# A state-space mixer with a quantized gate: the first chunk's norm token tile by token tile, the early loads in another order

## The chip, the cores and the metric

The kernel runs on one core of one Trainium2 chip. The core has five engines with queues of their own: TensorE (PE; PEld is its weight load), VectorE (DVE), ScalarE (ACT), GpSimd (POOL) and SyncE (SP), which here issues all DMA transfers of the program. The metric is the device time of one execution in microseconds (us), as the median of several runs.

## The reference

```python
xn = layernorm(x)                        # x is 1 x 2048 tokens x 1024
x_, gate = split(xn @ W_in.T)            # 2 x 2048 channels
u = silu(causal_conv4(x_) + conv_b)
ts, Bm, Cm = rms(split(u @ W_x.T))       # 64, 16 and 16 columns
dt = softplus(ts @ W_dt.T + b_dt)
state = state * exp(dt * A) + (dt * u) * Bm     # over the 2048 tokens, 16 states a channel
s = ((state . Cm) + u * D) * silu(gate) @ W_out.T
g = silu(ffn(xn))                        # int levels with scales, plus low rank gate_A, gate_B, ...
out = x + s * g
```

The change touches the layernorm of the first 512 tokens and the transfers around it. Everything behind is the same.

## The kernel before, in words

The kernel is written in raw instructions, one program for each engine, and each engine runs its program in the order in which it stands; semaphores (`f_...`, `z_...`) order engines against each other. SyncE's order of transfers is written out by hand. The program starts with a front part, up to about 549 us, and then a long scan.

The front part goes through four chunks of 512 tokens (four tiles of 128 tokens each) and in each chunk through 16 weight tiles of `W_in`; one (chunk, weight tile) is a unit, numbered u = 0 to 63, and every engine's loop runs over u. Before the loop, chunk 0 is prepared. VectorE takes the statistics of the four token tiles (`moments`), gathers them, and normalises (`scaled`) each tile; TensorE turns a tile in two halves (`turn_x`); ScalarE writes the turned half in half precision (`high`), and VectorE the rest that this leaves (`low`). `xn` has two buffers, the turned halves have two.

A weight tile w is loaded raw (`load_raw`, two buffers), scaled and rounded by ScalarE (`weight_high`, two instructions), its rest made by GpSimd (`weight_low`, counted in `f_lo`), used by TensorE in unit w, and stored to memory by SyncE (`store_w`), from where chunks 1 to 3 fetch it (`reload_w`). A raw buffer is free for tile w when `f_lo` says that w - 2 has been made. ScalarE's loop makes tile u + 2 first and then the tanh of unit u - 1; so a late raw tile also holds that tanh back. VectorE's loop is, for each u, `silu(u - 2)`, which waits for that tanh, then `conv(u - 1)`, then pieces for the next chunk's norm and the low-rank factors. The last instruction of a convolution adds three columns (L636). TensorE's loop is `unit(u)`, then `w_x(u - 2)`, which needs `silu(u - 2)`. GpSimd's `head` takes the seam between chunks from VectorE's convolutions, every fourth unit, ahead of `weight_low`.

SyncE's loop stores weight tile u + 2 and loads tile u + 4; at u = 0 it also loads x for chunk 1 (2 MB), at u = 14 it stores the low-rank factor table `b_s`, waits for it, and loads `wdt` behind it. The low-rank factors `lr_a` are loaded three times each (so many copies are needed side by side), `g_b` four times, each into 32 partitions.

In the profile's names, `dd` holds x and later `g_b` and `u_b`; `bb` holds `xn` and the raw weight tiles; `work` holds the converted weight tiles and the convolution's buffer; `inj` holds u, the constants and `lr_a`; `xtp_turned` are the turned halves, `main_decay` and `main_bank` the three result banks of the units; `xx` is the finished input of all units.

Of the kernel before, what the change touches and what calls it, by code (L numbers as in the profile page):

```python
# [27 lines left out]
ALU = mybir.AluOpType  # L28
# [3 lines left out]
P = 128  # L32
# [19 lines left out]
    "f_ds0 f_ds1 f_ww0 f_ww1 f_ww2 f_ws0 f_ws1 f_ws2 f_us0 f_us1 f_us2 f_dv f_ds2 f_tl "  # L52
# [30 lines left out]
def mixer_kernel(nc, x, win, convw, convb, wx, wdt, bdt, alog, dskip, wout, gu_q, g_scale, u_scale,  # L83
# [3 lines left out]
    with whole:  # L87
# [88 lines left out]
        with ExitStack() as st:  # L176
# [33 lines left out]
            rstd = sb(st, "rstd", [P, TPC, 1])  # L210
            bd = sb(st, "bd", [P, DT])
# [23 lines left out]
            f_us = [sem(f"f_us{b}") for b in range(3)]  # L235

# [41 lines left out]
            with nc.Block() as block:  # L278
                @block.sync
                def _(sp):  # L280
                    def load_x(c):
                        for half in range(2):
                            least(sp, f_xn, c * TPC - TPC + 2 * half + 2 if c else 0)
# [72 lines left out]
                    for w in range(2):  # L356
                        store_w(w)
                        load_raw(w + 2)
# [77 lines left out]
                def _(act):  # L436
# [8 lines left out]

                    def root(c):
                        act.wait_ge(f_nv, LEAD + 14 * c + 13)
                        act.activation(var[:, :, :], var[:, :, :], ACT.Sqrt).then_inc(f_sd, 1)
# [65 lines left out]
                    root(0)  # L514
                    for w in range(2):
                        weight_high(w)
                    for h in range(2 * TPC):
                        high(h)
                    for u in range(LAST + 2):
# [22 lines left out]
                        if u == 2:  # L542
                            act.wait_ge(f_const, LEAD + 112)
# [8 lines left out]
                        if u == 16:  # L552
                            act.wait_ge(f_const, LEAD + 144)
# [37 lines left out]
                def _(v):  # L591
                    def moments(c, t):
# [4 lines left out]
                    def gather(c):  # L597
                        v.wait_ge(f_nv, LEAD + 14 * c + 8)
                        for t in range(TPC):
                            v.bn_aggr(mv[:, t, :], stats[:, t, :, :].rearrange("p a s -> p (a s)")).then_inc(f_nv, 1)  # L600
                        v.wait_ge(f_nv, LEAD + 14 * c + 12)
                        v.tensor_scalar(var[:, :, :], mv[:, :, 1:2], 1e-5, None, ALU.add).then_inc(f_nv, 1)

                    def inverse(c):
                        v.wait_ge(f_sd, LEAD + c + 1)
                        v.reciprocal(rstd[:, :, :], var[:, :, :]).then_inc(f_nv, 1)

                    def scaled(c, t):
                        i = c * TPC + t
                        v.wait_ge(f_nv, LEAD + 14 * c + 14)  # L610
# [262 lines left out]
                def _(pe):  # L873
# [1126 lines left out]
```

## Time and profile before

| what | value |
|---|---|
| three runs | 2754.17, 2758.93, 2759.13 us |
| median | 2758.93 us |
| span of the profiled execution (first to last instruction) | 2757.4 us |
| busy over the span: TensorE, VectorE, GpSimd, ScalarE | 96%, 87%, 73%, 58% |
| mean granted clock of TensorE | 0.989 |

The profiled execution has no time of its own beside its span; the median stands 1.53 us above it, which is what lies around a span. Times in the rows count from the span's start. In a row of a timeline, the first number is the start, the second the time from the first to the last of the instructions that the row takes together, and what stands in brackets is how long the engine had been idle before, and what ended that.

### The profile page before, as it was taken

What the parts mean: (1) busy time and instruction counts of PE and PEld (TensorE: products, weight loads), DVE (VectorE), ACT (ScalarE), POOL (GpSimd) and SP (SyncE); (2) the same over time, 40 slices, a digit from 0 to 9 for tenths busy, and PEclk for the clock granted to TensorE, in tenths of its full rate; (3) what the DMA queues carried; (4) which work ended last, traced back from release to release, by engine and by line L of the source; (5) the groups of instructions that cost most, each with busy time, mean ns of one, the idle gap of its engine ahead of it and who ended that gap; (6) DMA issues with size and microseconds to landing.
All of it is one profiled execution on the core that took longest, in us unless ns stands there. A gap on an engine that the chain in (4) does not pass through costs nothing.

```text
span 2757.4 us, 41660 instructions
## 1 busy us (share of the span) xinstructions
PE 2653.1 (96%) x14980; PEld 1529.7 (55%) x14980; DVE 2392.3 (87%) x2900; ACT 1587.5 (58%) x2657; POOL 1999.2 (73%) x957
## 2 busy tenths in 40 slices
PE   6999999799999999999999999989999998999999
PEld 3545555355555555555555555556666665655644
DVE  5978877699999998888888888899999999999920
ACT  4444645666666666777777776655555555445500
POOL 2302223188999998888898988888999898999811
PEclk9999999899999999999999999999999999999999
DMA  7755476255565545454445445564565658666541
GB/s 246 239 173 193 141 268 210 100 161 177 157 194 172 161 135 160 130 156 138 150 124 166 130 126 161 169 198 120 156 157 133 165 128 254 163 175 192 149 128 58
DMA packets 338798, 449.10 MB, mean 163 GB/s; under 512 B 170592, under 2 KB 181088, under 8 KB 334496
## 3 DMA queue, kind: packets, MB, share of 16 engines
q1 hardware_dynamic: 338592, 446.43, 54.1%
q8 instruction: 120, 1.97, 0.3%
q14 instruction: 86, 0.70, 0.1%
HBM read 312.39 MB, written 133.96 MB: 162 GB/s over the span
## 4 chain that ended last, share of the span: by engine, by line
PE 34%; DVE 28%; issue 10%; DMA 3%; POOL 3%; ACT 1%; SPq 0%; DVEq 0%; POOLq 0%; ACTq 0%
DVE inj L1543 15%; DVE ysum L1563 9%; PE main_bank L1781 6%; PE main_bank L1783 6%; PE xtp_turned L1739 6%; PE main_bank L1857 4%; PE misc_bank L1781 3%; PE misc_bank L1783 3%; DMA h_s<-work 3%; PE misc_bank L1857 2%; POOL inj L1687 2%; DVE work L1597 1%; DMA gs_s<-work 1%; PE main_bank L1792 1%; DVE us L1572 1%
## 5 line engine op out<-in xcount | busy, mean ns | idle before, releaser
L1687 POOL TENSOR_TENSOR inj<-dd,bb 128x2048 f32<-128x2048 f32 x255 | 1156.4, 4535 | 181.0 <-PE xtp_turned L1739 179.7
L1739 PE MATMUL xtp_turned<-ident,inj 128*128 128x128 f32 x4096 | 626.3, 276 | 41.8 <-DVE inj L1543 31.1
L1543 DVE TENSOR_TENSOR_SCAN inj<-ssm_decay,carry,inj 128x512 f32<-128x512 f32 x512 | 655.8, 1281 | 4.1 <-ACT ssm_decay L1393 3.6
L1543 DVE TENSOR_TENSOR_SCAN inj<-main_decay,carry,inj 128x512 f32<-128x512 f32 x512 | 652.8, 1275 | 0.5 <-ACT main_decay L1393 0.3
L1739 PEld LDWEIGHTS xtp_turned<-ident,inj 128*128 128x128 f32 x4096 | 504.5, 142 | 253.0 <-DVE inj L1543 79.1
L1563 DVE SCALAR_TENSOR_TENSOR ysum<-xtp_turned,cT,ysum 128x512 f32<-128x512 f32 x707 | 522.6, 739 | 97.8 <-PE xtp_turned L1739 97.1
L1393 ACT ACTIVATE main_decay<-dd,aneg 128x512 f32<-128x512 f32 x511 | 351.1, 687 | 369.9 <-DVE inj L1543 369.5
L1393 ACT ACTIVATE ssm_decay<-dd,aneg 128x512 f32<-128x512 f32 x511 | 352.4, 690 | 282.7 <-DVE inj L1543 281.1
L1781 PE MATMUL main_bank<-xx,work 128*128 128x512 f16 x936 | 355.1, 379 | 2.4 <-ACT work L1406 2.4
L1783 PE MATMUL main_bank<-xx,work 128*128 128x512 f16 x936 | 355.2, 380 | 0.0
L1699 POOL TENSOR_TENSOR ysum<-ysum,work 128x512 f32<-128x512 f32 x239 | 306.2, 1281 | 10.5 <-ACT work L1439 10.5
L1762 PE MATMUL main_bank<-xx,work 128*128 128x512 f16 x960 | 234.8, 381 | 8.8 <-PEq L278 8.8
L894 PE MATMUL main_bank<-xx,work 128*128 128x512 f16 x1008 | 227.0, 382 | 4.3 <-DMA work<-w_s 4.1
L1439 ACT ACTIVATE work<-xtp_turned,cT 128x512 f32<-128x512 f32 x239 | 162.0, 678 | 63.9 <-POOL ysum L1699 39.6
L1857 PE MATMUL main_bank<-xx,work 128*128 128x512 f16 x768 | 186.0, 382 | 0.0
L1781 PE MATMUL misc_bank<-xx,work 128*128 128x512 f16 x472 | 179.3, 380 | 0.0
L1783 PE MATMUL misc_bank<-xx,work 128*128 128x512 f16 x472 | 179.1, 380 | 0.0
L894 PEld LDWEIGHTS main_bank<-xx,work 128*128 128x128 f16 x1008 | 97.6, 99 | 121.1 <-issue 8.2
L821 POOL TENSOR_TENSOR taps<-halo,inj 128x12 f32<-128x12 f32 x36 | 10.0, 304 | 200.5 <-DVE halo L633 200.5
L1762 PEld LDWEIGHTS main_bank<-xx,work 128*128 128x128 f16 x960 | 94.3, 98 | 88.8 <-issue 12.0
L1783 PEld LDWEIGHTS main_bank<-xx,work 128*128 128x128 f16 x936 | 91.7, 98 | 85.5 <-issue 0.3
L1781 PEld LDWEIGHTS main_bank<-xx,work 128*128 128x128 f16 x936 | 91.7, 98 | 85.4 <-ACT work L1406 2.6
(208 smaller groups left out, 3956.1 us busy)
## 6 DMA issues: line engine op xcount, KB each, us to landing
bb<-bt_s SPq DMA_DIRECT2D x128, 512.0 KB, 5.9
work<-w_s SPq DMA_DIRECT2D x48, 512.0 KB, 3.8
work<-in_gu_q SPq DMA_DIRECT2D x88, 256.0 KB, 3.4
h_s<-work SPq DMA_DIRECT2D x88, 256.0 KB, 3.8
u_s<-inj SPq DMA_DIRECT2D x64, 256.0 KB, 4.4
dd<-dt_s SPq DMA_DIRECT2D x32, 512.0 KB, 8.8
gs_s<-work SPq DMA_DIRECT2D x64, 256.0 KB, 6.1
us<-u_s SPq DMA_DIRECT2D x60, 256.0 KB, 5.4
```

Source lines behind the costliest of these rows:

```text
L894: mm = pe.matmul(main[u % 3][:, :], ww[:, u % 3, part, k * P:(k + 1) * P], xx[:, c, side, k, :], start=(k == 0 and part + side == 0), stop ...
L1393: act.activation(decay[j % 2][:, :], dtb[:, step % 2, j, :], ACT.Exp, scale=aneg[:, step % G * J + j, n:n + 1]).then_inc(s_dec, 1)
L1439: act.activation(ysum[:, step % 2, ADDS, :] if n == 0 else ev[:, :], turned[ADDS % 2][:, :], ACT.Copy, scale=cT[:, step // G * TPC + ADDS, ...
L1543: v.tensor_tensor_scan(inj[:, s % RING, j, :], decay[j % 2][:, :], inj[:, s % RING, j, :], carry[:, step % G * J + j, n:n + 1], ALU.mult, ...
L1563: v.scalar_tensor_tensor(dst, turned[t % 2][:, :], weight, dst, ALU.mult, ALU.add).then_inc(s_sum, 1)
L1687: pool.tensor_tensor(inj[:, e % RING, :, :], dub[:, step % 2, :, :], bb[:, e % 8:e % 8 + 1, :].broadcast_to([P, J, T]), ALU.mult).then_inc ...
L1699: pool.tensor_tensor(ysum[:, step % 2, ADDS, :], ysum[:, step % 2, ADDS, :], ev[:, :], ALU.add).then_inc(s_acc, 1)
L1739: mm = pe.transpose(turned[t % 2][:, j * P:(j + 1) * P], inj[:, s % RING, j, t * P:(t + 1) * P], ident[:, :])
L1762: mm = pe.matmul(bank[u % 3][:, :], gw[w % 2][:, part, h * P:(h + 1) * P], xx[:, c, side, h, :], start=(h == 0 and part + side == 0), stop ...
L1781: pe.matmul(dst[:, :], w, xx[:, p, 0, h, :], start=(h == 0), stop=False, skip_group_check=True)
L1783: mm = pe.matmul(dst[:, :], w, xx[:, p, 1, h, :], start=False, stop=False, skip_group_check=True)
L1857: mm = pe.matmul(bank[z % 3][:, :], y, (wo_hi, wo_hi, wo_lo)[w][:, i, half * T:(half + 1) * T], start=(i == 0 and w == 0), stop=(i == DT - ...
```

## The change

Chunk 0 is no longer normalised in one go. Its four tiles are loaded as two single tiles and a pair, each tile's mean and variance is taken when it has landed, and ScalarE normalises it, as x times the inverse deviation plus a shift, with VectorE making the shift (`first_...`). ScalarE's conversion of weight tile 0 stands between the tiles, that of tile 1 behind all of them. TensorE's first turn waits for the identity alone (`p_id`), not for all seven constants. In SyncE's order the low-rank loads `lr_a` stand in two groups around the first weight stores, and the `g_b` loads behind the load of raw tile 3. Chunks 1 to 3 are normalised as before; their counts are shifted by `NV0`.

```diff
-                    load_x(0)
-                    for w in range(2):
-                        load_raw(w)
-                    for dst, src in ((ident, ident_in), (wx_sb, wx), (cw, convw), (cb, convb), (bd, bdt), (al, alog),
-                                     (dsk, dskip)):
+                    load_first(0)
+                    load_first(1)
+                    sp.dma_start(ident[:], ident_in).then_inc(p_id, 16)
+                    load_raw(0)
+                    load_second()
+                    load_raw(1)
+                    for dst, src in ((cw, convw), (cb, convb), (bd, bdt), (al, alog), (dsk, dskip), (wx_sb, wx)):
                         sp.dma_start(dst[:], src).then_inc(f_const, 16)
-                    for m in range(2):
-                        for r in range(3):
-                            sp.dma_start(araw[:, m * HK:(m + 1) * HK, r * LR:(r + 1) * LR],
-                                         lr_a[m]).then_inc(f_a, 16)
+                    load_low_rank(0)
+                    store_w(0)
+                    load_raw(2)
+                    load_low_rank(1)
+                    store_w(1)
+                    load_raw(3)
                     for r in range(4):
                         sp.dma_start(braw[r * LR:(r + 1) * LR, :], g_b).then_inc(f_b, 16)
-                    for w in range(2):
-                        store_w(w)
-                        load_raw(w + 2)
...
+                    def first_scaled(t):
+                        act.wait_ge(f_nv, LEAD + first_done(t, "shift"))
+                        least(act, f_tp, 2 * t - 2)
+                        act.activation(xn[:, t % 2, :], xt[:, t, :], ACT.Identity, bias=shift[:, t, :],
+                                       scale=rstd[:, t, :]).then_inc(f_xn, 1)
...
-                    root(0)
-                    for w in range(2):
-                        weight_high(w)
-                    for h in range(2 * TPC):
-                        high(h)
+                    first_root(0)
+                    first_scaled(0)
+                    first_root(1)
+                    high(0)
+                    high(1)
+                    first_scaled(1)
+                    first_root(2)
+                    weight_high(0)
+                    high(2)
+                    high(3)
+                    first_scaled(2)
+                    first_root(3)
+                    high(4)
+                    high(5)
+                    first_scaled(3)
+                    high(6)
+                    high(7)
+                    weight_high(1)
...
-                    for t in range(TPC):
-                        moments(0, t)
-                    gather(0)
-                    inverse(0)
-                    scaled(0, 0)
-                    scaled(0, 1)
-                    for t in range(TPC):
-                        low(2 * t)
-                        low(2 * t + 1)
-                        if t + 2 < TPC:
-                            scaled(0, t + 2)
-                    v.wait_ge(f_const, LEAD + 112)
+                    first_moments(0)
+                    first_variance(0)
+                    for t in range(1, TPC):
+                        first_moments(t)
+                        first_inverse(t - 1)
+                        first_variance(t)
+                        if t > 1:
+                            low(2 * t - 4)
+                            low(2 * t - 3)
+                    first_inverse(TPC - 1)
+                    for h in range(2 * TPC - 4, 2 * TPC):
+                        low(h)
+                    v.wait_ge(f_const, LEAD + 96)
...
-                    pe.wait_ge(f_const, LEAD + 112)
+                    pe.wait_ge(p_id, LEAD + 16)
                     pe.wait_ge(f_z, LEAD + 1)
                     for h in range(2 * TPC):
                         turn_x(h)
+                    pe.wait_ge(f_const, LEAD + 96)
```

SyncE's queue, from the low-rank loads (`lr_a`, then `g_b`) to the load of raw weight tile 5, before; `w_s<-work` is a weight store, `bb<-in_win` a raw load:

```order
L352 DMA inj<-in_lr_a 128x8x32 x6
L355 DMA dd<-in_g_b 32x2816 x4
L294 DMA w_s<-work 128x2048 [waits f_lo]
L290 DMA bb<-in_win 128x1024 [waits f_lo]
L294 DMA w_s<-work 128x2048 [waits f_lo]
L290 DMA bb<-in_win 128x1024 [waits f_lo]
L294 DMA w_s<-work 128x2048 [waits f_lo]
L290 DMA bb<-in_win 128x1024 [waits f_lo]
L284 DMA dd<-in_x 128x2x1024 [waits f_xn] x2
L294 DMA w_s<-work 128x2048 [waits f_lo]
L290 DMA bb<-in_win 128x1024 [waits f_lo]
```

The same stretch of the changed kernel:

```order
L298 DMA inj<-in_lr_a 128x8x32 x3
L314 DMA w_s<-work 128x2048 [waits f_lo]
L310 DMA bb<-in_win 128x1024 [waits f_lo]
L298 DMA inj<-in_lr_a 128x8x32 x3
L314 DMA w_s<-work 128x2048 [waits f_lo]
L310 DMA bb<-in_win 128x1024 [waits f_lo]
L379 DMA dd<-in_g_b 32x2816 x4
L314 DMA w_s<-work 128x2048 [waits f_lo]
L310 DMA bb<-in_win 128x1024 [waits f_lo]
L304 DMA dd<-in_x 128x2x1024 [waits f_xn] x2
L314 DMA w_s<-work 128x2048 [waits f_lo]
L310 DMA bb<-in_win 128x1024 [waits f_lo]
```

The `g_b` loads have moved behind two weight stores and two raw loads that wait for `f_lo`, so they stand directly ahead of store 2, raw load 4, x of chunk 1, store 3 and raw load 5.

ScalarE ahead of its loop, before; L439 and L444 are the two instructions of `weight_high`, L453 is `high`:

```order
L448 ACTIVATE var<-var 128x4 [waits f_nv]
L439 ACTIVATE bb<-bb 128x1024 [waits f_w0]
L444 ACTIVATE work<-bb 128x1024 [waits f_sc]
L439 ACTIVATE bb<-bb 128x1024 [waits f_w1]
L444 ACTIVATE work<-bb 128x1024 [waits f_sc]
L453 ACTIVATE xx<-xtp_turned 128x4x128 [waits f_tp] x8
```

The changed kernel, from the normalising of token tile 1 (L474; L469 is the root) to the conversion of weight tile 1:

```order
L474 ACTIVATE bb<-dd,shift,rstd 128x1024 [waits f_nv]
L469 ACTIVATE rstd<-var 128x1 [waits f_nv]
L460 ACTIVATE bb<-bb 128x1024 [waits f_w0]
L465 ACTIVATE work<-bb 128x1024 [waits f_sc]
L484 ACTIVATE xx<-xtp_turned 128x4x128 [waits f_tp] x2
L474 ACTIVATE bb<-dd,shift,rstd 128x1024 [waits f_tp,f_nv]
L469 ACTIVATE rstd<-var 128x1 [waits f_nv]
L484 ACTIVATE xx<-xtp_turned 128x4x128 [waits f_tp] x2
L474 ACTIVATE bb<-dd,shift,rstd 128x1024 [waits f_tp,f_nv]
L484 ACTIVATE xx<-xtp_turned 128x4x128 [waits f_tp] x2
L460 ACTIVATE bb<-bb 128x1024 [waits f_w1]
L465 ACTIVATE work<-bb 128x1024 [waits f_sc]
```

Both weight conversions have moved from ahead of the turned halves to among and behind them.

## Rows read from the trace of the kernel before

**Rows 1.** Stretches: us; busy PE, PEld, DVE, ACT, POOL; clock; DMA share, GB/s.

```profile
54.00:120.00 66.00, 66.00 (x363) 37.47 (x362) 61.25 (x96) 40.43 (x45) 29.25 (x26) 1.00 0.70 229
120.00:150.00 30.00, 25.65 (x127) 13.56 (x125) 20.84 (x35) 5.37 (x8) 0.97 (x5) 0.89 0.89 290
150.00:480.00 330.00, 330.00 (x1713) 174.09 (x1712) 268.99 (x454) 171.63 (x218) 78.60 (x56) 1.00 0.59 192
```

**Rows 2.** Timeline, TensorE: start, us, line, output<-inputs, count, idle before.

```profile
19.02 1.97 PE L879 MATMUL xtp_turned<-ident,bb 128*128 128x128 f32 x8 [19.02 <-DMA dsk<-in_dskip]
...
30.27 7.25 PE L894 MATMUL main_decay<-xx,work 128*128 128x512 f16 x24 [1.51 <-DVE xx L619]
...
79.01 5.34 PE L894 MATMUL main_bank<-xx,work 128*128 128x512 f16 x24
...
141.58 7.92 PE L894 MATMUL main_bank<-xx,work 128*128 128x512 f16 x24 [4.13 <-DMA work<-w_s]
```

**Rows 3.** Timeline, SyncE's queue, the DMA issues.

```profile
10.28 10.10 SPq L352 DMA_DIRECT2D inj<-in_lr_a  x6
20.42 2.18 SPq L355 DMA_DIRECT2D dd<-in_g_b  x4
...
37.20 0.33 SPq L294 DMA_DIRECT2D w_s<-work  x1
...
41.23 0.56 SPq L290 DMA_DIRECT2D bb<-in_win  x1
...
122.28 0.32 SPq L298 DMA_DIRECT2D work<-w_s  x1
...
130.75 1.37 SPq L396 DMA_DIRECT2D inj<-in_wdt  x2
132.16 0.92 SPq L298 DMA_DIRECT2D work<-w_s  x1
```

**Rows 4.** Timeline, GpSimd, weight subtraction.

```profile
70.85 2.13 POOL L809 TENSOR_TENSOR work<-bb,work 128x1024 f16<-128x1024 f32 x1 [5.50 <-ACT work L444]
...
115.28 4.22 POOL L809 TENSOR_TENSOR work<-bb,work 128x1024 f16<-128x1024 f32 x2
```

**Rows 5.** Timeline, VectorE.

```profile
9.82 5.04 DVE L595 BATCH_NORM_STATS2 stats<-dd 128x6 f32<-128x512 f32 x8 [4.62 <-DMA dd<-in_x]
...
29.43 0.69 DVE L619 TENSOR_TENSOR xx<-xtp_turned,xx 128x512 f16<-128x512 f32 x1 [0.16 <-ACT xx L453]
...
54.02 0.69 DVE L643 SCALAR_TENSOR_TENSOR inj<-main_bank,work 128x512 f32<-128x512 f32 x1 [2.74 <-ACT main_bank L458]
...
71.02 1.98 DVE L636 TENSOR_TENSOR work<-work,corr 128x3 f32<-128x3 f32 x1
...
76.14 0.69 DVE L643 SCALAR_TENSOR_TENSOR inj<-main_bank,work 128x512 f32<-128x512 f32 x1
```

**Rows 6.** Timeline, ScalarE.

```profile
15.56 0.20 ACT L448 ACTIVATE var<-var 128x4 f32<-128x4 f32 x1 [9.74 <-DVE var L602]
...
20.17 0.60 ACT L453 ACTIVATE xx<-xtp_turned 128x512 f16<-128x512 f32 x1 [0.33 <-PE xtp_turned L879]
21.02 0.60 ACT L453 ACTIVATE xx<-xtp_turned 128x512 f16<-128x512 f32 x1 [0.26 <-PE xtp_turned L879]
...
41.88 1.06 ACT L439 ACTIVATE bb<-bb 128x1024 f32<-128x1024 f32 x1 [0.26 <-DMA bb<-in_win]
...
51.27 1.06 ACT L439 ACTIVATE bb<-bb 128x1024 f32<-128x1024 f32 x1 [3.41 <-DMA bb<-in_win]
...
53.40 0.58 ACT L458 ACTIVATE main_bank<-work 128x512 f32<-128x512 f32 x1
```

**Rows 7.** Stretches, columns as in the first group: the `g_b` loads, then plain loads.

```profile
22.00:28.50 6.50, 5.20 (x24) 3.92 (x22) 4.55 (x7) 2.94 (x5) 0.10 (x1) 1.00 1.06 225
30.00:34.00 4.00, 3.73 (x9) 1.31 (x10) 0.39 (x4) 1.14 (x2) 0.00 (x0) 1.00 1.02 418
```

**Rows 8.** One stretch, line 636 alone: us, VectorE's busy time, clock, DMA.

```profile
54.00:120.00 66.00, 5.97 (x10) 1.00 0.70 229
```

More of the change, by code:

```diff
@@ L210, in mixer_kernel @@
             rstd = sb(st, "rstd", [P, TPC, 1])
+            shift = sb(st, "shift", [P, TPC, 1])
             bd = sb(st, "bd", [P, DT])
@@ L235, in mixer_kernel, with first_done @@
             f_us = [sem(f"f_us{b}") for b in range(3)]
+            p_id, p_x = sem("p_id"), sem("p_x")
+            def first_done(t, what):
+                last = 6 * t + 5 + 2 * (t < TPC - 1)
+                return {"stats": 6 * t, "mean": 6 * t + 3, "var": 6 * t + 4, "inverse": last, "shift": last + 1}[what]
+            NV0 = first_done(TPC - 1, "shift")
             def least(eng, s_, count):
@@ L280, in _, with load_first, load_second, load_low_rank @@
                 def _(sp):
+                    def load_first(t):
+                        sp.dma_start(xt[:, t, :], x[t]).then_inc(f_x[t], 16)
+                    def load_second():
+                        sp.dma_start(xt[:, 2:4, :], x[2:4].rearrange("t p h -> p t h")).then_inc(p_x, 16)
+                    def load_low_rank(m):
+                        for r in range(3):
+                            sp.dma_start(araw[:, m * HK:(m + 1) * HK, r * LR:(r + 1) * LR],
+                                         lr_a[m]).then_inc(f_a, 16)
                     def load_x(c):
                         for half in range(2):
-                            least(sp, f_xn, c * TPC - TPC + 2 * half + 2 if c else 0)
+                            least(sp, f_xn, c * TPC - TPC + 2 * half + 2)
                             sp.dma_start(xt[:, 2 * half:2 * half + 2, :],
@@ L444, in weight_high, with first_root @@
                         act.activation(ww[:, w % 3, 0, :], wraw[:, w % 2, :], ACT.Copy).then_inc(f_hi, 1)
+                    def first_root(t):
+                        act.wait_ge(f_nv, LEAD + first_done(t, "var"))
+                        act.activation(rstd[:, t, :], var[:, t, :], ACT.Sqrt).then_inc(f_sd, 1)
+                    def first_scaled(t):
[3 more added lines that the diff above has]
+                                       scale=rstd[:, t, :]).then_inc(f_xn, 1)
                     def root(c):
-                        act.wait_ge(f_nv, LEAD + 14 * c + 13)
+                        act.wait_ge(f_nv, LEAD + NV0 + 14 * (c - 1) + 13)
                         act.activation(var[:, :, :], var[:, :, :], ACT.Sqrt).then_inc(f_sd, 1)
@@ L552, in _ @@
                         if u == 16:
-                            act.wait_ge(f_const, LEAD + 144)
+                            act.wait_ge(f_const, LEAD + 128)
                             act.wait_ge(f_bs, LEAD + 48)
@@ L591, in _, with first_moments, first_variance, first_inverse @@
                 def _(v):
+                    def first_moments(t):
+                        v.wait_ge(f_x[t] if t < 2 else p_x, LEAD + 16)
+                        for h in range(2):
+                            v.bn_stats(stats[:, t, h, :], xt[:, t, h * 512:(h + 1) * 512]).then_inc(f_nv, 1)
+                    def first_variance(t):
+                        v.wait_ge(f_nv, LEAD + max(2, first_done(t, "stats")))
+                        v.bn_aggr(mv[:, t, :], stats[:, t, :, :].rearrange("p a s -> p (a s)")).then_inc(f_nv, 1)
+                        v.wait_ge(f_nv, LEAD + first_done(t, "mean"))
+                        v.tensor_scalar(var[:, t, :], mv[:, t, 1:2], 1e-5, None, ALU.add).then_inc(f_nv, 1)
+                    def first_inverse(t):
+                        v.wait_ge(f_sd, LEAD + t + 1)
+                        v.reciprocal(rstd[:, t, :], rstd[:, t, :]).then_inc(f_nv, 1)
+                        v.wait_ge(f_nv, LEAD + first_done(t, "inverse"))
+                        v.tensor_scalar(shift[:, t, :], mv[:, t, 0:1], rstd[:, t, :], -1.0, ALU.mult, ALU.mult
+                                        ).then_inc(f_nv, 1)
                     def moments(c, t):
@@ L609, in scaled @@
                         i = c * TPC + t
-                        v.wait_ge(f_nv, LEAD + 14 * c + 14)
+                        v.wait_ge(f_nv, LEAD + NV0 + 14 * (c - 1) + 14)
                         least(v, f_tp, 2 * i - 2)
```

10 lines of the change are left out of this document (5 added, 5 removed).

## Prediction

> **What bounds the kernel now.** I read the table of stretches first, because this change touches only the first microseconds and the question is whether their end is handed on. From 150 to 480 us TensorE is busy for all 330 us [rows 1], so what lies behind 150 us starts as early or as late as TensorE gets into that stretch, and a shift there goes to the end one for one. Between 54 and 120 us TensorE is also busy throughout, but VectorE is busy for 61.25 of 66 us [rows 1]. Two engines look like the limit at once, and which of them is decides this case.
>
> The TensorE rows tell. Unit 0 (the first weight tile) starts at 30.27, and unit 17 at 141.58 after 4.13 us of waiting for the weight tile that `reload_w` fetches [rows 2]. So TensorE arrives early there; its lead is thrown away. I then followed what that reload waited for, backwards. In SyncE's queue it is issued at 132.16, behind the `wdt` loads at 130.75, which wait for the `b_s` stores, which stand behind the first reload at 122.28 [rows 3]; that one waits until all 16 weight tiles are stored, and the last two are made by GpSimd at 115.28 to 119.50, right behind `head` [rows 4], whose input is a VectorE convolution. So the chain runs through VectorE, and it is VectorE's pace from 54 us on that sets unit 17, not TensorE's.
>
> Where does VectorE's full stretch begin? At 54.02, after 2.74 us of idling for ScalarE's tanh of unit 2 [rows 5]. That tanh, at 53.40, stands on ScalarE behind `weight_high(5)`, which began at 51.27 after 3.41 us of waiting for the load of raw tile 5 [rows 6]. So the transfer that lands at 51.27 starts the chain. It was issued at 41.23, and with it queued, from 37.20 on, two stores, two weight loads and the 2 MB of x for chunk 1 [rows 3].
>
> **The change, step by step.** *The head.* Before, 1 MB of x had landed at 9.82 and eight statistics took 5.04 us [rows 5]. A 0.52 MB tile at the 418 GB/s of a full read stretch [rows 7] is 1.25 us less: tile 0 at 8.57. Two statistics 1.26, aggregate and variance 0.4, root 0.20 [rows 6], then, behind tile 1's statistics on VectorE, reciprocal and shift near 11.95. Normalising on ScalarE is a 128x1024 operation not in the trace in this form; the nearest is the copy with a scale at 1.06 [rows 6]; two 128x512 operations of 0.60 [rows 6] give 1.20 from above, and nothing cheaper of that size is there. I take 1.05. So TensorE turns the first half tile at 13.05, not 19.02 [rows 2]; the constants it waited for are no longer in its way.
>
> From there ScalarE sets the pace, since it now normalises, converts and makes weight tile 0 between. A turned half is ready 1.15 us after its start and a second 0.85 later (19.02 to 20.17 to 21.02 [rows 2, 6]): high(0) and high(1) 14.2 to 15.65, normalise tile 1 to 16.7, root 16.9, `weight_high(0)` two operations, 19.05; high(2), high(3) 20.25; tile 2 21.3, root 21.5; turned halves at 22.5 and 23.35, done 23.95; tile 3 25.0; halves from 26.15, done 27.6. VectorE's low part is 0.69 [rows 5]: unit 0 starts near 28.45, 1.8 us earlier. The second x transfer (behind 0.59 MB more, at the latest 13.75) is covered. The new 128x1 operations are under 0.2 us each and lie in this sum.
>
> *What moved behind it.* `weight_high(1)` now stands after high(7): 27.6 to 29.75, GpSimd's 2.13 [rows 4] to 31.95. Only then may SyncE issue `store_w(1)` and the load of raw tile 3, and behind them the four `g_b` loads, which in the old queue were issued at 20.42 [rows 3]. Store and load of a tile on an idle queue took from 37.20 to 41.88, 4.68 us [rows 3, 6]: raw tile 3 lands at 36.65. ScalarE and GpSimd make tile 3 of it by 41.1; before, `store_w(3)` and load 5 began with 41.23, so their place in the queue is the same.
>
> But the queue is longer. The `g_b` copies are 4 x 352 KB into 32 partitions each; the stretch in which they move has the engines full at 225 GB/s, where full-width transfers have 418 [rows 7]: 1.44 MB / 0.225 = 6.4 us. Before, they were done while TensorE still turned chunk 0. Now they move between load 3 and the chain's five transfers. These took 51.27 - 37.20 = 14.07 us with an empty queue, of which some 2.05 are issue and landing (4.68 less 1.05 MB at about 0.4): 12.0 of moving. Load 5 lands at 36.65 + 6.4 + 12.0 = 55.05 instead of 51.27: **+3.8 us**.
>
> *Handed on.* Tanh of unit 2 at 57.2, VectorE's full stretch from 57.8. VectorE has at most 66 - 61.25 = 4.75 us of gaps in its 66 [rows 1], mostly its wait for the tanh of the unit it has just convolved, so it does not catch up. ScalarE's and GpSimd's weight tiles, and the loads behind them, follow VectorE's units; unit 17 moves by the same 3.8. TensorE's 1.8 us of lead is used up: its `w_x(5)` after unit 7, just ahead of unit 8 at 79.01 and with silu(5) done at 76.83 [rows 2, 5], now waits until 80.6, and unit 8 starts near 81.6. Nothing else is lost, as its margin to unit 17 is 4.13 us.
>
> The small rest costs nothing at the end: three low-rank loads each ahead of `store_w(0)` and `store_w(1)` are issued while those wait (all six took 10.10 us of issue [rows 3], three of them fit between 22.1 and 31.95); the constants land long before unit 0; VectorE loses four normalisations, but before 28 us.
>
> Sum: -1.8 at unit 0, not handed on; +6.4 for `g_b` in the chain's queue, less 2.6 by which the way is free earlier (37.20 + 2.05 for issue and landing, against 36.65); net +3.8 us. The profiled execution spans 2757.4 us, 1.53 under the median of the three runs, 2758.93; I add the difference to the median: **2762.7 us**, +0.14%. What a measurement of this kernel can tell is about 0.2%, 5.5 us; so my forecast counts as no change.
>
> **Bounds.** `g_b` at the full 418 GB/s would be 3.4 us: the sum is then +0.8. If normalising is 1.20 and tile 0 lands only with the whole megabyte, the head is 1.7 us later, and the sum +5.5.
>
> **Rivals.** *The lead arrives.* If transfers from different requests share the engines instead of following each other, load 5 is not late, tanh 2 follows convolution 2, and the start's 1.8 us go through: 2757.1. Against it: load 4, with 2 MB of x issued right behind it, still landed by 41.88, 4.68 us after the store ahead of it was issued [rows 3, 6], and load 5, behind the 2 MB, took until 51.27. Chance 0.13.
>
> *The clock pays back.* The wait before unit 17 is followed by half clock: that unit took 7.92 us where a unit at full clock takes 5.34 [rows 2], and the granted clock of the stretch is 0.89 [rows 1]. If the new wait at unit 8 already drops the clock to 1.2 GHz, TensorE arrives at unit 17 with less to wait, and the drop there may not come: 3.8 - 2.6 = +1.2, 2760.1. Chance 0.13.
>
> *Slower.* VectorE's three-column addition L636 takes 0.16 us, but 1.98 at 71.02, ending at 73.00, when GpSimd's weight subtraction from 70.85 ends (72.98) [rows 4, 5]. Ten of them between 54 and 120 us take 5.97 [rows 8], 4.4 over 10 x 0.16. Since loads now land at other times, the subtractions can meet more of the additions; from 1.7 us more on (one full meeting) the kernel is over 0.2% slower, and twice the meetings give 3.8 + 4.4 = +8.2, 2767.1. Against it: both sides hang on VectorE's units, so the meetings should recur. Chance 0.17, and the same rows allow -0.6 if there are none. The Trainium skill, "SBUF — State Buffer", section "Who interferes with whom", says a VectorE instruction with two SBUF inputs and a GpSimd instruction that reads SBUF lock each other out, the later one blocked until the first has ended. By that rule each addition issued inside a subtraction waits for its end, so that the sum hangs on the offset alone; the trace agrees, with 73.00 against 72.98.
>
> **How the numbers follow.** Forecast +3.8: 0.54; the other three as given; 0.03 for anything else. Its own range is 2759.7 to 2764.4 from the bounds. Eight in ten need the clock and the start rival and half the lock's reach, and the runs' own spread (2754.17 to 2759.13): 2755.5 to 2767.5. Faster by over 0.2% needs the start's gain and no meeting at all: 0.05. Slower by over 0.2%: the lock's 0.17 and the forecast's upper edge, 0.23. Same: 0.72.
>
> **What would show it.** Right: unit 0 at 27.5 to 29.5; ScalarE waits for raw tile 5 until 54 to 56; a TensorE wait behind unit 7; unit 17 near 145.4. Wrong: load 5 at or before 51.3, with `g_b` beside it; unit 17 earlier than 141.58; or a unit 0 after 30, which would mean that ScalarE's row in the head is longer than I made it.

## The result and the profile after

| | before | changed |
|---|---|---|
| median, 22 runs each on the same chip | 2758.62 us | 2763.91 us |
| lowest to highest | 2753.18 to 2764.01 us | 2758.68 to 2769.92 us |
| span of the profiled execution | 2757.4 us | 2757.8 us |
| mean granted clock of TensorE | 0.989 | 0.989 |

The ratio is 1.002, 95% interval 1.0013 to 1.0027: 5.3 us slower, at the edge of what was called no change. The forecast was 2762.7 us, +3.8, and lies inside the interval too. The two spans differ by 0.4 us only; below it is read what became of the difference in them. All medians and ratios here and in the experiments leave out the five slow executions of the later sessions, which took from 4202 to 13432 us.

The changed kernel's timeline of TensorE, with the columns of [rows 2]: two of the four turnings of the head, unit 0, the `w_x` ahead of unit 8, units 8, 17 and 63:

```profile
12.93 1.94 PE L942 MATMUL xtp_turned<-ident,bb 128*128 128x128 f32 x8 [12.93 <-ACT bb L474]
17.93 1.97 PE L942 MATMUL xtp_turned<-ident,bb 128*128 128x128 f32 x8 [3.06 <-ACT bb L474]
...
29.41 7.86 PE L957 MATMUL main_decay<-xx,work 128*128 128x512 f16 x24 [1.50 <-DVE xx L681]
...
81.24 1.13 PE L968 MATMUL ssm_decay<-work,inj 128*128 128x96 f32 x8 [2.67 <-DVE inj L705]
82.21 7.03 PE L957 MATMUL main_bank<-xx,work 128*128 128x512 f16 x24
...
146.65 7.04 PE L957 MATMUL main_bank<-xx,work 128*128 128x512 f16 x24 [4.12 <-DMA work<-w_s]
...
477.76 5.34 PE L957 MATMUL main_decay<-xx,work 128*128 128x512 f16 x24
```

Against [rows 2] the first turning is 6.1 us earlier, unit 0 only 0.86, unit 8 3.2 us later and unit 17 5.07 later. Unit 63, the last of the front part, is the best place to see what is handed on; before, it stood here:

```profile
473.57 5.34 PE L894 MATMUL main_decay<-xx,work 128*128 128x512 f16 x24
```

That is 4.19 us and not 5.07, since unit 17 took 7.04 us, not 7.92: less of it ran at half clock (granted clock 0.76 over the unit, 0.66 before).

ScalarE's timeline of the changed kernel, as [rows 6]: the normalising of tiles 0 and 1, raw weight tiles 3 and 5, the tanh of unit 2, raw tile 13:

```profile
11.55 1.24 ACT L474 ACTIVATE bb<-dd,shift,rstd 128x1024 f32<-128x1024 f32 x1 [1.30 <-DVE shift L651]
...
16.63 1.24 ACT L474 ACTIVATE bb<-dd,shift,rstd 128x1024 f32<-128x1024 f32 x1 [1.13 <-DVE shift L651]
...
39.02 1.06 ACT L460 ACTIVATE bb<-bb 128x1024 f32<-128x1024 f32 x1 [6.41 <-DMA bb<-in_win]
...
55.54 1.06 ACT L460 ACTIVATE bb<-bb 128x1024 f32<-128x1024 f32 x1 [3.95 <-DMA bb<-in_win]
...
57.68 0.58 ACT L489 ACTIVATE main_bank<-work 128x512 f32<-128x512 f32 x1
...
106.24 1.06 ACT L460 ACTIVATE bb<-bb 128x1024 f32<-128x1024 f32 x1 [0.96 <-DMA bb<-in_win]
```

Raw tile 5 lands at 55.54 where it landed at 51.27, and the tanh stands right behind its conversion, as before. VectorE, as [rows 5]: the statistics of token tile 2, the shift of tile 1 and silu of unit 2:

```profile
15.00 1.29 DVE L639 BATCH_NORM_STATS2 stats<-dd 128x6 f32<-128x512 f32 x2 [3.19 <-DMA dd<-in_x]
16.20 0.15 DVE L649 RECIPROCAL rstd<-rstd 128x1 f32<-128x1 f32 x1
16.38 0.21 DVE L651 TENSOR_SCALAR shift<-mv,rstd 128x1 f32<-128x1 f32 x1
...
58.29 0.69 DVE L705 SCALAR_TENSOR_TENSOR inj<-main_bank,work 128x512 f32<-128x512 f32 x1 [3.59 <-ACT main_bank L489]
```

SyncE's queue, as [rows 3]: store 1, load 3, `g_b`, store 2; then the reload of unit 16, the second `b_s` store, `wdt`, the reload of unit 17:

```profile
32.81 0.33 SPq L314 DMA_DIRECT2D w_s<-work  x1
33.18 0.43 SPq L310 DMA_DIRECT2D bb<-in_win  x1
33.66 2.26 SPq L379 DMA_DIRECT2D dd<-in_g_b  x4
35.96 0.66 SPq L314 DMA_DIRECT2D w_s<-work  x1
...
127.48 0.33 SPq L318 DMA_DIRECT2D work<-w_s  x1
...
128.95 0.66 SPq L414 DMA_DIRECT2D b_s<-ab  x1
135.97 1.38 SPq L417 DMA_DIRECT2D inj<-in_wdt  x2
137.39 1.01 SPq L318 DMA_DIRECT2D work<-w_s  x1
```

The stretches, with the columns of [rows 1]:

```profile
54.00:120.00 66.00, 63.00 (x335) 34.79 (x335) 57.77 (x92) 40.65 (x45) 25.17 (x23) 0.97 0.73 236
120.00:150.00 30.00, 25.46 (x132) 13.85 (x131) 25.82 (x42) 7.66 (x11) 5.48 (x9) 0.95 0.81 253
150.00:480.00 330.00, 330.00 (x1710) 173.84 (x1709) 267.95 (x450) 168.78 (x216) 75.43 (x55) 1.00 0.59 194
```

TensorE now has 3.0 us of idling between 54 and 120 us, and from 150 to 480 it is full again: the shift of 4.19 is carried through it unchanged. Behind it the two profiled executions differ, and no row shows why. After a wait of 1.07 us near 490 the execution of before got half clock for a few products (0.57 granted from 491 to 495 us), and six of them took 2.74 us; the changed one took 1.47 for the same six and made up 1.6 us there. Before:

```profile
491.25 0.38 PE L927 MATMUL misc_back<-inj 128*128 128x512 f16 x1 [1.07 <-DVE inj L676]
491.56 0.61 PE L928 MATMUL misc_back<-inj 64*128 64x512 f16 x1
492.10 2.74 PE L940 MATMUL xtp_turned<-xx,a 128*128 128x512 f16 x6
```

Of the kernels below only one (`w1_early`) drops there too. That leaves 2.57 us at the first GpSimd product of the scan (551.78 us, 549.21 before), and the scans take up most of that, so that the spans end 0.4 us apart. A single pair of spans is therefore no measure of a change of this size; the medians are.

### The profile page after: what moved, and what is told of

Same layout as the page of the kernel before. It is cut to its first block, busy times and chain, and to the rows that moved or that the text cites. A ratio compares the mean times of both kernels' runs of the same rounds, so it can differ in the third digit from the quotient of the medians.

```text
span 2757.8 us, 41676 instructions
## 1 busy us (share of the span) xinstructions
PE 2654.5 (96%) x14980; PEld 1530.6 (56%) x14980; DVE 2392.1 (87%) x2906; ACT 1591.7 (58%) x2664; POOL 1999.3 (72%) x957
## 4 chain that ended last, share of the span: by engine, by line
PE 34%; DVE 29%; issue 11%; POOL 3%; DMA 3%; ACT 1%; DVEq 0%; SPq 0%; POOLq 0%; ACTq 0%
DVE inj L1607 15%; DVE ysum L1627 9%; PE main_bank L1845 6%; PE main_bank L1847 6%; PE xtp_turned L1803 6%; PE main_bank L1921 4%; PE misc_bank L1847 3%; PE misc_bank L1845 3%; DMA h_s<-work 2%; PE misc_bank L1921 2%; POOL inj L1751 2%; DVE work L1661 1%; PE main_bank L1856 1%; DVE us L1636 1%; DVE xa L1672 1%
```

## The experiments

My theory after the result: the `g_b` loads in the queue of raw tiles 4 and 5 make raw tile 5 late, this holds the tanh of unit 2 and with it VectorE, and VectorE's lateness goes through the weight stores to unit 17. Rivals: that the late start of the head or of weight tile 1 is what counts, or the place of `g_b` alone, or that unit 17 would be late anyway. All experiments ran in three sessions, each with runs of the kernel before; its medians there were 2757.09 us (35 runs), 2755.84 (32) and 2757.07 (27). Each experiment has 10 or 11 runs. The last three columns are starts in the profiled execution (of raw tile 5, that of its conversion on ScalarE). The ratio is to the runs of before in the same session; kernels of different sessions are compared by it and not by their medians.

| kernel | median us | ratio to before, interval | raw tile 5 | unit 17 | unit 63 |
|---|---|---|---|---|---|
| before | 2758.62 | | 51.27 | 141.58 | 473.57 |
| changed | 2763.91 | 1.002 [1.0013, 1.0027] | 55.54 | 146.65 | 477.76 |
| gb_early | 2756.81 | 0.9999 [0.999, 1.0007] | 49.93 | 140.68 | 472.47 |
| old_gb_late | 2755.51 | 0.9995 [0.9986, 1.0003] | 48.50 | 139.38 | 470.66 |
| gb_wide | 2759.53 | 1.0008 [1.0, 1.0017] | 53.16 | 144.22 | 475.24 |
| tanh_first | 2760.38 | 1.0013 [1.0004, 1.0022] | 55.67 | 143.97 | 475.54 |
| w1_early | 2756.69 | 1.0001 [0.9992, 1.001] | 51.15 | 142.26 | 474.29 |
| pair_first | 2762.02 | 1.0016 [1.0007, 1.0025] | 55.22 | 145.64 | 476.39 |
| reload_early | 2761.88 | 1.0024 [1.0015, 1.0034] | 54.98 | 141.22 | 478.61 |
| three | 2757.74 | 1.0005 [0.9996, 1.0014] | 52.20 | 137.25 | 473.28 |
| wdt_late | 2758.49 | 1.0008 [0.9999, 1.0017] | 55.80 | 142.20 | 474.75 |
| gb_wdt | 2753.76 | 0.9992 [0.9983, 1.0001] | 49.85 | 137.13 | 469.91 |
| old_wdt | 2754.97 | 0.9993 [0.9984, 1.0002] | 51.36 | 137.13 | 469.51 |

The starts are those of one execution each. `tanh_first`, `reload_early` and `wdt_late` have the same transfers as the changed kernel up to raw tile 5, and there it starts at 55.67, 54.98 and 55.80: less than 1 us between two kernels shows nothing in that column.

**gb_early.** The changed kernel with `g_b` back ahead of the first weight store, all else as changed.

```diff
                     load_low_rank(0)
+                    for r in range(4):
+                        sp.dma_start(braw[r * LR:(r + 1) * LR, :], g_b).then_inc(f_b, 16)
                     store_w(0)
...
                     load_raw(3)
-                    for r in range(4):
-                        sp.dma_start(braw[r * LR:(r + 1) * LR, :], g_b).then_inc(f_b, 16)
```

> The changed kernel with the four g_b loads moved forward in SyncE's queue, directly behind the first low-rank loads and ahead of store_w(0). Theory (g_b stands in the way of the five transfers whose last one is raw tile 5): g_b is then moved before 29 us, raw tile 5 lands near 49.5 instead of 55.54, tanh of unit 2 near 51.5 to 52, no TensorE wait behind unit 7 of more than 1 us, unit 17 at 139 to 141 instead of 146.65, and the time 5 to 7 us under the changed kernel's, 0 to 2 us under the kernel before. Rival (the head alone is at fault, since ScalarE makes weight tile 1 only behind the last turned half, so that every later weight tile is late): raw tile 5 still lands after 54, unit 17 stays at 145 to 147, and the time stays 4 to 6 us above the kernel before.

The whole loss is gone with this one line's place. ScalarE's timeline in it, raw tile 5 and the tanh of unit 2:

```profile
49.93 1.06 ACT L460 ACTIVATE bb<-bb 128x1024 f32<-128x1024 f32 x1 [1.63 <-DMA bb<-in_win]
...
52.07 0.58 ACT L489 ACTIVATE main_bank<-work 128x512 f32<-128x512 f32 x1
```

Raw tile 5 lands 5.61 us earlier than in the changed kernel, unit 17 is 5.97 earlier, unit 63 5.29, although unit 0 starts at 29.99, 0.58 later than in the changed kernel. So what the head gains does not reach unit 17, and what the queue loses does.

**old_gb_late.** The kernel before with `g_b` behind the load of raw tile 3, that is, only this part of the change.

```diff
-                    for r in range(4):
-                        sp.dma_start(braw[r * LR:(r + 1) * LR, :], g_b).then_inc(f_b, 16)
                     for w in range(2):
                         store_w(w)
                         load_raw(w + 2)
+                    for r in range(4):
+                        sp.dma_start(braw[r * LR:(r + 1) * LR, :], g_b).then_inc(f_b, 16)
```

> The kernel before with one edit alone: the four g_b loads stand behind the load of raw tile 3, as in the changed kernel. There that load is issued at 24.6 us and not after 32.8. Theory (only bytes that are still in the queue when store 2 is issued count): raw tiles 2 and 3 land about 5 us earlier, g_b is moved from 29 to 35.5, ahead of the chain's transfers, which are issued from about 34 instead of 37.2; raw tile 5 lands at 48 to 50 instead of 51.27, unit 17 at 139 to 141 instead of 141.58, the time 0 to 2.5 us under the kernel before. Rival (the place behind raw tile 3 costs g_b's 6.4 us whatever the head is): raw tile 5 at 54 to 56, unit 17 at 145 to 147, the time 4 to 6 us above the kernel before.

So the place in the order of the program doesn't cost by itself. Here weight tiles 0 and 1 are made early, the `g_b` loads are issued at 23.19 and have moved before store 2 is issued at 33.80. The loss needs both: `g_b` behind raw tile 3, and weight tile 1 made late, so that `g_b` is issued at 33.66, 2.3 us ahead of store 2. Raw tile 5 is converted here without a wait, and the tanh of unit 2 waits for its convolution, not for a transfer. Raw tiles 2 and 3 are converted 3.4 and 2.3 us earlier than before (29.44 and 32.97), not the 5 expected. ScalarE, raw tile 5 and the tanh:

```profile
48.50 1.04 ACT L439 ACTIVATE bb<-bb 128x1024 f32<-128x1024 f32 x1
...
52.98 0.60 ACT L458 ACTIVATE main_bank<-work 128x512 f32<-128x512 f32 x1 [2.26 <-DVE work L636]
```

**w1_early.** The changed kernel with the conversion of weight tile 1 right behind that of tile 0.

```diff
                     weight_high(0)
+                    weight_high(1)
...
                     high(7)
-                    weight_high(1)
```

> The changed kernel with one edit on ScalarE: the conversion of weight tile 1 stands right behind that of tile 0, between the turned halves of token tile 0 and 1, instead of behind the last half. SyncE's order is as it was. Theory (what counts is when g_b's bytes leave the queue ahead of the chain's transfers): store_w(1), raw load 3 and g_b are issued from about 27 instead of 32.8, g_b is through by 38 instead of 43, raw tile 5 lands at 50 to 51.5, unit 17 at 140.5 to 142.5 instead of 146.65, and the time is 4 to 6 us under the changed kernel's, although unit 0 starts 1.5 to 2.1 us later (31 to 31.5). Rival (TensorE's start is what is handed on): unit 17 and the time move with unit 0, 1.5 to 2 us later than in the changed kernel.

This is the plainest of the runs. Unit 0 starts at 31.79, 2.4 us later than in the changed kernel and 1.5 later than before, and the kernel is still as fast as before. Store 1 is issued at 27.30 and `g_b` at 28.47 instead of 33.66, and raw tile 5 lands at 51.15 (51.27 before). TensorE's early start is not handed on; the place in the queue is. Unit 0 and raw tile 5 in it:

```profile
31.79 6.88 PE L957 MATMUL main_decay<-xx,work 128*128 128x512 f16 x24 [1.50 <-DVE xx L681]
```
```profile
51.15 1.06 ACT L460 ACTIVATE bb<-bb 128x1024 f32<-128x1024 f32 x1 [1.85 <-DMA bb<-in_win]
```

**gb_wide.** The changed kernel, with `g_b` stored four times over in memory, prepared outside the kernel, and loaded as four column pieces into 128 partitions each: as many bytes and as many transfers as in the changed kernel, but full width.

```diff
-                        sp.dma_start(braw[r * LR:(r + 1) * LR, :], g_b).then_inc(f_b, 16)
+                        cut = slice(r * IPAD // 4, (r + 1) * IPAD // 4)
+                        sp.dma_start(braw[:, cut], g_b[:, cut]).then_inc(f_b, 16)
```

> The changed kernel with g_b repeated four times in memory by the host and loaded in four column pieces into all 128 partitions, the same 1.44 MB and the same place in the queue. Theory (32 partitions are why g_b moves at 225 GB/s): it moves at 380 to 420 GB/s in 3.4 to 3.8 us instead of 6.4, raw tile 5 lands 2.6 to 3 us earlier (52.5 to 53), unit 17 at 143.5 to 144.5, the time 2.5 to 3.5 us under the changed kernel's. Rival (g_b is slow for another reason, such as the mixture of stores and loads around it): no change, raw tile 5 near 55.5, unit 17 near 146.6.

ScalarE's timeline in it, raw tiles 3 and 5:

```profile
37.49 1.06 ACT L461 ACTIVATE bb<-bb 128x1024 f32<-128x1024 f32 x1 [5.01 <-DMA bb<-in_win]
...
53.16 1.06 ACT L461 ACTIVATE bb<-bb 128x1024 f32<-128x1024 f32 x1 [3.94 <-DMA bb<-in_win]
```

Of the 5.61 us that `g_b` costs raw tile 5, 2.38 are due to the 32 partitions; the bounds of the prediction (6.4 and 3.4) had 3.0 for it. Between 38 and 43 us, behind raw tile 3, the transfers run at 340 GB/s here; the changed kernel has 211 from 38 to 43.5. The Trainium skill, "SBUF — State Buffer", section "Door 1: The DMA port swizzle (why `[64,N]` ≈ `[32,N]`)", says that partitions 0 to 31 reach 8 of the 16 ports and gives about 218 GB/s for them, 436 for all; the trace agrees, with 225 and 418 [rows 7].

**pair_first.** The changed kernel with the second x transfer (token tiles 2 and 3) ahead of raw weight tile 0.

```diff
-                    load_raw(0)
                     load_second()
+                    load_raw(0)
                     load_raw(1)
```

> The changed kernel with the pair of token tiles 2 and 3 loaded ahead of raw weight tile 0 instead of behind it. Theory (ScalarE's row in the head waits for the statistics of tile 2, which wait for the pair, and its end sets weight tile 1, g_b and the chain one for one): VectorE's wait for the pair ends 1 to 1.4 us earlier (13.6 to 14 instead of 15.00), unit 0 starts 1 to 1.4 earlier, raw tile 5 lands 1 to 1.4 earlier and unit 17 too (145.2 to 145.7); the time 1 us under the changed kernel's, too little to tell by the clock. Rival (the head has slack toward the chain): raw tile 5 and unit 17 where they were.

VectorE's statistics of tile 2 and ScalarE's raw tile 5:

```profile
14.12 1.29 DVE L639 BATCH_NORM_STATS2 stats<-dd 128x6 f32<-128x512 f32 x2 [2.34 <-DMA dd<-in_x]
```
```profile
55.22 1.06 ACT L460 ACTIVATE bb<-bb 128x1024 f32<-128x1024 f32 x1 [3.94 <-DMA bb<-in_win]
```

The statistics come 0.88 us earlier, and unit 0 by the same 0.88 (28.53). That shows the pair of x as a limit of the head: in every kernel but `w1_early`, whose ScalarE has another order there, unit 0 starts 14.4 us after these statistics. But raw tile 5 is only 0.32 earlier, less than executions differ by with the same transfers, and not the 1 to 1.4 expected; unit 17 is 1.0 earlier, and the time is not measurably better.

**tanh_first.** The changed kernel, with ScalarE's tanh ahead of the weight conversion in units 1 to 3, so that a late raw tile doesn't hold it.

```diff
-                        if u + 2 < DT:
+                        if u + 2 < DT and not 1 <= u <= 3:
...
+                        if 1 <= u <= 3:
+                            weight_high(u + 2)
```

> The changed kernel with one edit on ScalarE: in the loop's steps 1 to 3 the tanh of unit u - 1 stands ahead of the conversion of weight tile u + 2, so a late raw tile 4 or 5 no longer holds the tanh back. No transfer moves. Theory (the loss comes through the tanh to VectorE): VectorE's full stretch begins near 52 instead of 58.29 although raw tile 5 still lands near 55.5; TensorE then sets the pace; unit 17 at 139.5 to 142, the time 4 to 6 us under the changed kernel's. Rival (the late weight tiles themselves hold TensorE, the tanh is beside the point): unit 17 stays at 145 to 147, and the time stays as it was.

ScalarE in it, the tanh of unit 2, raw tile 5, the tanh of unit 3:

```profile
52.59 0.60 ACT L489 ACTIVATE main_bank<-work 128x512 f32<-128x512 f32 x1 [1.40 <-DVE work L700]
...
55.67 1.06 ACT L460 ACTIVATE bb<-bb 128x1024 f32<-128x1024 f32 x1 [2.48 <-DMA bb<-in_win]
...
61.29 0.58 ACT L489 ACTIVATE main_decay<-work 128x512 f32<-128x512 f32 x1
```

The tanh of unit 2 is 5.09 us earlier, with raw tile 5 as late as in the changed kernel. So it was this tile that held it. But the next tanh then stands behind the late conversions of tiles 5 and 6, and silu of unit 3, at 64.10 in the changed kernel, starts at 61.91: 2.19 us of the gain are left, and 2.68 at unit 17. In time it is about half of the 4 to 6 us that were expected. The lateness is of the transfer and its conversion, and moving the tanh only passes part of it by.

**reload_early and three.** `reload_early` is the changed kernel with the reload of unit 17 ahead of the `b_s` stores and `wdt`; `three` adds the edits of `gb_early` and `tanh_first`.

```diff
-                            reload_w(u + 2)
+                            if u + 2 != DT + 1:
+                                reload_w(u + 2)
...
                         if u == 14:
+                            reload_w(DT + 1)
```

> The changed kernel with the load of unit 17's weight tile issued ahead of the stores of b_s, so that it doesn't stand behind SyncE's wait for them and behind the 1 MB of wdt. Theory (the only place before 480 us where TensorE waits for this chain is unit 17): the wait of 4.12 us goes, unit 17 starts near 142.5, at full clock (5.34 us instead of 7.04), and the time falls by 4.1 + 1.7 = 5.8 us, to 0 to 1 us above the kernel before. Rival (something else behind it waits for the same chain, such as unit 18's tile or the dt products with wdt): the wait returns at unit 18 or 19 with 2 us or more, and less than 3 us is gained.

> Three edits of the experiments together on the changed kernel: g_b loads behind the first low-rank loads, tanh ahead of the weight conversion in steps 1 to 3, unit 17's reload ahead of the b_s stores. Theory: each takes away one place where the chain runs, so TensorE's lead reaches the scan: VectorE's full stretch begins near 52, no wait over 1 us at unit 17, unit 17 near 137, and the time 5 to 8 us under the kernel before, clearly faster than both. Rival (VectorE, which is full from 54 to 120 us, keeps unit 17 where it is): 1 to 2 us under the kernel before, no more than the early g_b alone gave.

TensorE in `reload_early`, unit 18:

```profile
152.33 8.02 PE L959 MATMUL main_decay<-xx,work 128*128 128x512 f16 x24 [4.91 <-DMA work<-w_s]
```

Unit 17 starts without a wait at 141.22, 5.4 us earlier, and unit 18 then waits 4.91 us for its own reload, which still stands behind `wdt` and 2 MB of x. Unit 63 is even 0.85 later than in the changed kernel. `three` does the same (4.99 us at unit 18) and ends where `gb_early` does, not the 5 to 8 us under the kernel before that were expected. One reload moved past the obstacle moves the wait by one unit.

**wdt_late, gb_wdt and old_wdt.** The obstacle itself moved: the wait for `b_s`, the `wdt` loads and x for chunk 2 go behind the reload of unit 18, and ScalarE and VectorE make `wd` one unit later. `wdt_late` is that on the changed kernel, `gb_wdt` on `gb_early`, `old_wdt` on the kernel before.

```diff
-                        if q == 15 and 1 <= c + 1 < C - 1:
-                            load_x(c + 2)
+                        if u in (DT, 2 * DT - 1):
+                            load_x(2 if u == DT else 3)
...
                         if u == 14:
                             sp.wait_ge(f_bl, LEAD + 4)
...
+                        if u == 16:
                             sp.wait_ge(f_bs, LEAD + 48)
...
-                        if u == 16:
+                        if u == 17:
                             act.wait_ge(f_const, LEAD + 128)
...
-                        if u == DT + 1:
+                        if u == DT + 2:
                             v.wait_ge(f_ap, LEAD + 10)
```

> The changed kernel, with the wdt loads (and the wait for the b_s stores ahead of them) and the 2 MB of x for chunk 2 moved behind the reload of unit 18 in SyncE's queue; ScalarE and VectorE make wd one unit later. Theory: unit 17 starts late because its reload stands in SyncE's queue behind the wait for the b_s stores (128.95 to 135.97) and the next one behind wdt and x; with these out of the way the DMA wait of 4.12 us at unit 17 goes and does not come back at unit 18. Unit 17 then starts right behind unit 16, near 142 instead of 146.65, at full clock, the scan about 4 to 5 us earlier, the time about 2759.5, ratio to the kernel before 1.000 to 1.001. Rival: the wait comes back, at unit 18 as in reload_early, or at unit 17 on another transfer, because the weight tiles are only stored at 127.5 and the reloads need that long: then 2762 to 2765, ratio 1.002.

> gb_early with the same move of the wdt loads and of x for chunk 2. Theory: the two gains add, since one moves VectorE's pace up to unit 15 and the other the queue behind it: unit 17 near 136.5 to 137.5, the scan near 542, the time 4 to 5 us under gb_early, 2751 to 2753, ratio 0.998 to 0.999. Rival: the wait for the reloads comes back at unit 17 or 18: no better than gb_early, 2756 to 2758, ratio 1.000.

> The kernel before with the same move of the wdt loads and of x for chunk 2, nothing else. Theory: the wait of 4.13 us at unit 17, which is there before the change too, goes: unit 17 near 137.5, 2753 to 2755, ratio 0.998 to 0.999. Rival: it comes back one unit later: 2757 to 2760, ratio 1.000.

TensorE in `wdt_late`, units 17 and 19 and the turning of the small sums, and then its stretches from 120 us on:

```profile
142.20 5.34 PE L958 MATMUL main_bank<-xx,work 128*128 128x512 f16 x24
...
155.46 5.35 PE L958 MATMUL main_bank<-xx,work 128*128 128x512 f16 x24 [0.79 <-DMA work<-w_s]
...
163.62 0.66 PE L977 MATMUL misc_back<-ident,work 128*128 128x128 f32 x4 [1.95 <-DVE work L733]
```
```profile
120.00:150.00 30.00, 29.09 (x159) 16.37 (x158) 24.98 (x44) 7.00 (x11) 5.36 (x8) 1.00 0.90 280
150.00:480.00 330.00, 327.26 (x1693) 172.14 (x1692) 267.62 (x451) 173.67 (x219) 77.40 (x56) 1.00 0.60 195
```

The wait at unit 17 is gone and doesn't come back at unit 18; the clock between 120 and 150 us is 1.00 instead of 0.95. But 2.74 us return behind it: 0.79 at unit 19, and 1.95 for VectorE's sums (L733), a wait that neither the changed kernel nor the kernel before has. At unit 63, 3.0 us are left of the 4.45 at unit 17. `gb_wdt` keeps 2.56 of 3.55 against `gb_early`, and `old_wdt` 4.06 of 4.45 against the kernel before. In time, `gb_wdt` and `old_wdt` have the lowest ratios of all, but their intervals, 0.9983 to 1.0001 and 0.9984 to 1.0002, reach 1. That is 0.0008 and 0.0007 where 0.001 to 0.002 were expected, and not told apart from the kernel before.

The three together also show that the reload is not the only way by which the lateness reaches unit 17. In none of them does unit 17 wait for its reload, and still it starts at 142.20 in `wdt_late`, 5.07 later than in `gb_wdt` and `old_wdt`. There the lateness is in TensorE's own row: against `old_wdt`, unit 8 is 3.5 us late behind a wait of 2.82 us for VectorE, and shorter waits bring the rest by unit 16. TensorE in `old_wdt`, unit 17:

```profile
137.13 5.34 PE L895 MATMUL main_bank<-xx,work 128*128 128x512 f16 x24
```

## Why the prediction was right, and where it was off

The forecast of +3.8 us, "no change that can be told", came out as +5.3. Step by step:

- **The head: -1.8 us at unit 0.** It was -0.86 (29.41, not 28.45). Two terms were mis-sized. "The second x transfer ... is covered" was wrong: it landed at 15.00 and not by 13.75, and the normalising of tile 1 had to wait until 16.63, because VectorE makes its shift only behind the statistics of tile 2, which stand in VectorE's queue waiting for that transfer. `pair_first` shows it: 0.88 earlier there, 0.88 at unit 0. And normalising took 1.24 us, not 1.05, above even the upper bound of 1.20. The Trainium skill, "ScalarE: Activation LUTs", section "What ACT_TABLE_LOAD costs", has the price that my estimate left out: about 93 ns more for each operand that is given per partition. With two of them on the 1.04 of the plain copy that is 1.23, an estimate by that page; the trace agrees, with 1.24.
- **Raw tile 3 at 36.65.** It was 39.02. The store ahead of it was issued at 32.81, 0.86 later than forecast; the rest is that the load took 5.84 us from issue to landing, against 4.50 in `gb_early` and 4.45 in `gb_wide`, where no narrow transfer stands right behind it. I had let transfers follow each other without loss. Not all of the rest is that: with the same transfers the load took 4.85 us in `reload_early` and 4.88 in `wdt_late`, so about 1 us of the 5.84 belongs to this execution.
- **Raw tile 5 at 55.05, `g_b` 6.4 us of it.** It was 55.54, and `gb_early` puts `g_b` at 5.61. This step carried the forecast, and it was right in mechanism and near in size; two errors cancel in it, raw tile 3 2.37 later and the way from there to raw tile 5 1.88 shorter than I made it. That raw tile 5 came out within 0.5 us of the forecast is therefore in part luck.
- **Handed on: tanh at 57.2, VectorE's stretch from 57.8, a wait behind unit 7, unit 8 at 81.6.** 57.68, 58.29, a wait of 2.67 us, 82.21: right, each 0.5 to 0.6 us later, as raw tile 5 is.
- **Unit 17 moves by the same 3.8.** It moved by 5.07: 0.5 from raw tile 5, and 0.7 at raw tile 13, which ScalarE waited 0.96 us for (106.24) where it waited 0.27 before. In `reload_early` and `wdt_late`, whose transfers are the same up to there, it waited 0 and 0.29 us; so these 0.7 may be of this execution and not of the change. The rest of the chain held: GpSimd's last two weight tiles are 5.1 us later, the reload of unit 16 5.2. "Nothing else is lost, as its margin to unit 17 is 4.13 us" did not hold: TensorE begins unit 8 3.2 us later than before, unit 9 4.88 and unit 16, at 136.32, 5.08. That is more than the margin, and it does not show only because the reload is as late.
- **From there one for one.** Right, less 0.88 by which unit 17 ran faster: 4.2 us at units 18 and 63. The medians and the shift of unit 63 agree within 1.1 us for the change itself; over all kernels the times lie 0.1 to 3.4 us above what unit 63 says. That is one execution against medians, and it is not settled further. As all twelve lie above, the one profiled execution of before, against which all are counted, may itself have been late.

The rivals: *the lead arrives* is out: raw tile 5 was late by 4.27 us, and `w1_early` is as fast as the kernel before with no lead at all. *The clock pays back* holds for a part of its size: unit 8 ran at half clock for a time (7.03 us against 5.34, granted clock 0.52 from 82.2 to 85.7 us), but unit 17 still waited 4.12 us, and only 0.88 came back, not 2.6. Behind waits of 2.82, 2.62 and 2.55 us at the same place, `wdt_late`, `reload_early` and `pair_first` ran unit 8 at full clock, so even that part comes and goes. *Slower by the lock* is out: VectorE's ten additions took 5.76 us between 54 and 120 us, and 5.97 before [rows 8]. But the argument against it, that the meetings should recur, does not hold in general: ten such additions in the same stretch took 3.20 us in `reload_early` and 6.53 in `w1_early`.

## What to carry to other kernels

A start that is made earlier is worth nothing unless the thing that is late next is earlier too: here TensorE could start 1.5 us later than before at no cost (`w1_early`), while a load that nobody needed yet, issued 2 us ahead of the transfers that pace the kernel, cost all of the loss. When work is moved, follow each transfer behind it in its queue to the first engine that has no slack, and put what is not urgent where the queue is idle. And to remove a wait in such a queue, move the obstacle and not one of the things behind it, for the next one then waits instead.

## What the runs showed of the hardware

- A load that was issued ahead of a narrow one took longer: raw tile 3 took 4.8 to 5.8 us from issue to landing in the five kernels with the 32-partition `g_b` right behind it (5.84 in the changed kernel), 4.45 with `g_b` in 128 partitions, and 4.4 to 4.5 in the three changed kernels that issue `g_b` early.
- A wait of 2.67 us of TensorE ahead of `w_x(5)` was followed by half clock in unit 8 (7.03 us for 24 products instead of 5.34; granted clock 0.52 from 82.2 to 85.7 us). Waits of 2.82, 2.62 and 2.55 us at the same place in `wdt_late`, `reload_early` and `pair_first` were not (5.34 us, 1.00). Behind waits of 0.65 and 1.07 us near 490 us it dropped in two kernels' profiled executions, and not in the others, with the same rows around them. Waits of 1.34 and 1.68 us at units 17 and 18 of `old_gb_late` were followed by full clock (1.00 from 136 to 155 us).
